# Graph network kernel: the first aggregation's low parts of the counts, replaced by two rows found on the chip

## What is computed

```python
h = jnp.maximum(_layernorm(x, axis=-1), 0.0)
x = x + _L1_gnn_ref(h, edge_index, W_l, b_l, W_r, gamma, beta)
# in it:
agg = jax.ops.segment_sum(x[src], dst, num_segments=n)
cnt = jax.ops.segment_sum(jnp.ones((src.shape[0],), x.dtype), dst, num_segments=n)
mean_agg = agg / jnp.maximum(cnt, 1.0)[:, None]
h = mean_agg @ W_l.T + b_l + x @ W_r.T
```

## Time and profile before

| | us |
|---|---|
| median of 3 runs | 393.89 |
| lowest, highest | 393.66, 395.64 |
| profiled execution, span | 394.1 |
| TensorE busy | 374.8 (95%) |
| VectorE busy | 312.1 (79%) |
| ScalarE busy | 171.6 (44%) |
| GpSimd busy | 4.2 (1%) |

### The profile page before, as it was taken

How to read it: one execution, slowest core, us unless ns; L and a number is a source line. 1 busy time by engine, 2 the same in 40 slices (tenths; PEclk the granted TensorE clock), 3 DMA queues, 4 the chain that set the end, 5 groups by cost and what they waited for, 6 DMA issues and landing times.

```text
span 394.1 us, 5108 instructions
## 1 busy us (share of the span) xinstructions
PE 374.8 (95%) x1786; PEld 282.2 (72%) x1786; DVE 312.1 (79%) x660; ACT 171.6 (44%) x287; POOL 4.2 (1%) x19
## 2 busy tenths in 40 slices
PE   2989999999999999999999999999999999999994
PEld 1545566666657888887678788887588878787773
DVE  5889999999848789897868976698875788388236
ACT  5664666563044234244559533262363530145410
POOL 4000000000000000000000000000000000000000
PEclk9999999999999999999999999999999999999988
DMA  7602444343135000068200512200600050000002
GB/s 238 250 1 69 152 154 141 105 153 112 52 112 183 1 2 0 2 215 315 111 2 1 172 43 101 114 0 0 211 4 0 2 180 33 2 0 0 2 12 94
DMA packets 16360, 32.92 MB, mean 84 GB/s; under 512 B 1360, under 2 KB 1488, under 8 KB 16336
## 3 DMA queue, kind: packets, MB, share of 16 engines
q1 hardware_dynamic: 15744, 32.25, 23.9%
q10 hardware_dynamic: 592, 0.36, 0.3%
HBM read 21.07 MB, written 1.05 MB: 56 GB/s over the span
## 4 chain that ended last, share of the span: by engine, by line
PE 77%; DVE 14%; ACT 4%; issue 2%; DMA 1%; DVEq 0%; ACTq 0%
PE acc L1395 11%; PE bank L1377 10%; PE bank L1480 7%; PE bank L1270 6%; PE bank L1271 6%; PE bank L1251 4%; PE acc L1251 4%; PE acc L1271 4%; PE acc L1270 4%; PE bank L1465 3%; PE acc L1451 3%; DVE big_rounded L652 2%; PE acc L1228 2%; PE bank L1228 2%; PE acc L1545 2%
## 5 line engine op out<-in xcount | busy, mean ns | idle before, releaser
L1395 PE MATMUL acc<-wide_rounded,c_rounded 128*126 128x512 f32 x200 | 59.5, 439 | 0.7 <-ACT acc L464 0.7
L1395 PEld LDWEIGHTS acc<-wide_rounded,c_rounded 128*126 128x126 f32 x200 | 36.9, 186 | 19.8 <-issue 13.0
L792 DVE TENSOR_SCALAR wide_rounded<-iota_f,picked 128x512 fp32r<-128x512 f32 x100 | 42.2, 480 | 1.5 <-issue 1.1
L483 ACT COPY z_sb<-acc 126x512 f32<-126x512 f32 x37 | 21.6, 585 | 42.0 <-PE acc L1395 33.3
L507 ACT ACTIVATE wide<-wide,low_col 128x512 f32<-128x512 f32 x32 | 21.3, 715 | 32.9 <-DVE low_col L905 32.8
L1480 PEld LDWEIGHTS bank<-v_sb,big 128*128 128x128 f32 x256 | 29.7, 192 | 4.7 <-issue 4.0
L625 DVE TENSOR_TENSOR wslot_rounded<-wslot,wide_rounded 128x512 fp32r<-128x512 f32 x24 | 16.2, 687 | 21.2 <-ACT wslot L377 21.2
L1480 PE MATMUL bank<-v_sb,big 128*128 128x65 f32 x256 | 31.6, 277 | 0.0
L798 DVE TENSOR_TENSOR c_rounded<-row_bc,wslot_rounded 128x1008 fp32r<-128x1008 bf16 x25 | 30.0, 1201 | 0.0
L1377 PE MATMUL bank<-t_sb,wslot 128*128 128x512 f32 x64 | 29.5, 594 | 0.5 <-ACT t_sb L459 0.5
L652 DVE TENSOR_TENSOR big_rounded<-big,big_rounded 128x1024 fp32r<-128x1024 f32 x24 | 29.1, 1221 | 0.5
(11 more groups left out here) (312 smaller groups left out, 769.6 us busy)
## 6 DMA issues: line engine op xcount, KB each, us to landing
big<-z_sb SPq DMA_DIRECT2D x36, 252.0 KB
big<-in_w SPq DMA_DIRECT2D x4, 2048.0 KB, 7.8
x_sb<-in_x SPq DMA_DIRECT2D x8, 256.0 KB, 4.6
big<-in_w_3t SPq DMA_DIRECT2D x2, 1024.0 KB, 6.7
row_bc<-in_rows SPq DMA_DIRECT2D x7, 256.0 KB, 6.4
wslot<-in_wq SPq DMA_DIRECT2D x1, 1024.0 KB, 8.9
wslot<-in_wk SPq DMA_DIRECT2D x1, 1024.0 KB, 10.7
wslot<-in_wv SPq DMA_DIRECT2D x1, 1024.0 KB, 12.8
```

Source lines behind the costliest of these rows:

```text
L483: nc.scalar.copy(stage[0:BROWS, b % STAGES, :], a).then_inc(S["staged"], 1)
L792: nc.vector.tensor_scalar(hot_ring[:, u, k, :], iota_f[:, :], picked[:, 0, s0 + k:s0 + k + 1], None, ALU.is_equal)
L1395: last = nc.tensor.matmul(to, st_ring[:, u, 2 * k + a, :, :].rearrange("p w k -> p (w k)"), hot_ring[:, u, k, :], start=False, stop=False, ...
```

## The change

A count below 4096 is exact in its rounded high part, so its low part is zero; since there are 8192 edges, at most two nodes can have a row in `c1` with a larger count. The change finds the numbers of these two rows on the chip and multiplies only their low parts. VectorE takes the largest count of each row (four maxima over 128x512) within the loop over `f`, and forms from them, with two tables of row numbers, one column for the first and one for the last such row. TensorE turns the two columns into rows, between the first and the second bank of `ff2` (`most_turn`). VectorE makes two distinct row numbers from 0 to 511 of them (`heavy_rows`, between the split of the counts and the loop over `t`). SyncE has stored the counts in a tensor in DRAM; it loads the two numbers into registers and fetches the two rows of counts. VectorE waits for them and splits them in parts, ahead of its loop over `t`. SyncE stores each high part of `h` in DRAM too, as it is made, and fetches the same two rows of it; GpSimd copies them, and TensorE adds four multiplies with two rows at the end of the aggregation, in place of 16 with 128 rows at its start. The fetches stand in SyncE's queue ahead of the load of `w1_2`. Ten new semaphores aside, this is the diff:

```diff
...
 TINY = 1e-37
+HEAVY, EXACT = 2, 4096
+assert (HEAVY + 1) * EXACT > E
...
         rcnt_sb = sb("rcnt_sb", [P, N])
+        most = sb("most", [P, NT])
+        row_no = sb("row_no", [P, HEAVY, NT])
+        heavy_no = sb("heavy_no", [P, HEAVY])
+        heavy_f = sb("heavy_f", [1, 2 * HEAVY])
+        heavy_i = sb("heavy_i", [1, HEAVY], I32)
         steps = rcnt_sb[:, 0:1 + SLOTS]
...
         c2_hi = t_lo
+        heavy_c, heavy_hi = row_bc[0:HEAVY, 0, :], row_bc_r[0:HEAVY, 1, :]
+        heavy_lo, heavy_h = row_bc_r[0:HEAVY, 2, :], row_bc_r[0:HEAVY, 1, :]
+        counts_kept = nc.dram_tensor("counts_kept", (N, N), F32, kind="Internal").ap()
+        highs_kept = nc.dram_tensor("highs_kept", (N, D), F32, kind="Internal").ap()
         c2_lo = both(lambda a: a[:, 0, :, :], wslot, wslot_r)
...
             load("w2_0", w2_0)
+            for t in range(NT):
+                sp.dma_start(counts_kept[t * P:(t + 1) * P, :], c1[:, t, :]).then_inc(S["counts_out"], 16)
             sp.wait_ge(S["ff1_mm"], FT)
...
             load("w_lr", wr_t, 1)
+            sp.wait_ge(S["heavy_ready"], 1)
+            _, heavy_rows = nc.values_load_multi_w_load_instructions(
+                heavy_i[0:1, :], engines=[mybir.EngineType.SP], min_val=0, max_val=N - 1,
+                skip_runtime_bounds_check_because="a row's number, bounded where it is made on the chip")
+            sp.wait_ge(S["counts_out"], 16 * NT)
+            for i in range(HEAVY):
+                sp.dma_start(heavy_c[i:i + 1, :], counts_kept[bass.ds(heavy_rows[i], 1), :]
+                             ).then_inc(S["heavy_c_in"], 16)
+            by, before_these, _, _ = parts["h1"]
+            for t in range(NT):
+                sp.wait_ge(S[by], before_these + t + 1)
+                sp.dma_start(highs_kept[t * P:(t + 1) * P, :], z_sb_r[:, t, :].bitcast(F32)).then_inc(S["highs_out"], 16)
+            sp.wait_ge(S["highs_out"], 16 * NT)
+            sp.wait_ge(S["heavy_parts"], 2)
+            for i in range(HEAVY):
+                sp.dma_start(heavy_c[i:i + 1, :], highs_kept[bass.ds(heavy_rows[i], 1), :]
+                             ).then_inc(S["heavy_h_in"], 16)
             sp.wait_ge(S["ff2_mm"], NT)
...
                            allow_small_or_imprecise_dtypes=True).then_inc(S["tables"], 2)
+            nc.gpsimd.iota(row_no[:, 0, :], [[P, NT]], base=1, channel_multiplier=1,
+                           allow_small_or_imprecise_dtypes=True).then_inc(S["row_numbers"], 1)
+            nc.gpsimd.iota(row_no[:, 1, :], [[-P, NT]], base=N, channel_multiplier=-1,
+                           allow_small_or_imprecise_dtypes=True).then_inc(S["row_numbers"], 1)
             nc.gpsimd.iota(need_c[:, :], [[0, 1]], base=-NBK, channel_multiplier=1,
...
                            allow_small_or_imprecise_dtypes=True).then_inc(S["tables"], 1)
+            pool.wait_ge(S["heavy_h_in"], 16 * HEAVY)
+            nc.gpsimd.tensor_copy(heavy_h, heavy_c).then_inc(S["heavy_h_ready"], 1)
         @block.scalar
...
+            def heavy_rows():
+                first, second = heavy_f[:, 0:1], heavy_f[:, 1:2]
+                same, other = heavy_f[:, 2:3], heavy_f[:, 3:4]
+                dve.wait_ge(S["most_turned"], 1)
+                link(nc.vector.tensor_reduce(heavy_f[:, 0:HEAVY],
+                                             bank[0][0:1, 0:HEAVY * P].rearrange("p (a n) -> p a n", a=HEAVY),
+                                             AX.X, ALU.max))
+                mark(nc.vector.tensor_scalar(first, first, -1.0, 0.0, ALU.add, ALU.max))
+                link(nc.vector.tensor_scalar(second, second, -1.0, float(N), ALU.mult, ALU.add))
+                link(nc.vector.tensor_single_scalar(second, second, float(N - 1), ALU.min))
+                mark(nc.vector.tensor_tensor(same, first, second, ALU.is_equal))
+                link(nc.vector.tensor_scalar(other, first, float(N // 2), -float(N), ALU.is_ge, ALU.mult))
+                link(nc.vector.scalar_tensor_tensor(out=other, in0=other, scalar=float(N // 2), in1=same,
+                                                    op0=ALU.add, op1=ALU.mult))
+                link(nc.vector.tensor_tensor(second, second, other, ALU.add))
+                nc.vector.tensor_copy(heavy_i[:, :], heavy_f[:, 0:HEAVY]).then_inc(S["heavy_ready"], 1)
             def on_diagonal(to, column):
...
                     weight_lo("w2_0", f - 2, f - 1)
+                    mark(nc.vector.tensor_reduce(most[:, f - 2:f - 1], c1[:, f - 2, :], AX.X, ALU.max))
+                elif f == 6:
+                    settle()
+                    dve.wait_ge(S["row_numbers"], HEAVY)
+                    link(nc.vector.scalar_tensor_tensor(
+                        out=row_no[:, :, :], in0=most[:, :].unsqueeze(1).broadcast_to([P, HEAVY, NT]),
+                        scalar=float(EXACT), in1=row_no[:, :, :], op0=ALU.is_ge, op1=ALU.mult))
+                    nc.vector.tensor_reduce(heavy_no[:, :], row_no[:, :, :], AX.X, ALU.max).then_inc(S["most_ready"], 1)
             settle()
...
                                         ALU.subtract).then_inc(S["c1_parts_ready"], 1)
+            heavy_rows()
+            dve.wait_ge(S["heavy_c_in"], 16 * HEAVY)
+            nc.vector.tensor_copy(heavy_hi, heavy_c).then_inc(S["heavy_parts"], 1)
+            dve.wait_ge(S["heavy_parts"], 1)
+            nc.vector.tensor_tensor(heavy_lo, heavy_c, heavy_hi.bitcast(F32), ALU.subtract
+                                    ).then_inc(S["heavy_parts"], 1)
...
                     last.then_inc(S[done], 1)
+                    if m == 0 and between:
+                        between()
...
             pe.wait_ge(S["ff1_ready"], NT)
+            def most_turn():
+                pe.wait_ge(S["most_ready"], 1)
+                pe.wait_ge(S["ff1_ready"], NT + 1)
+                for i in range(HEAVY):
+                    last = nc.tensor.transpose(bank[0][0:1, i * P:(i + 1) * P], heavy_no[:, i:i + 1], ident[:, :])
+                last.then_inc(S["most_turned"], 1)
             product_in_parts(hi, halves(wide_at, wide_lo, FT), weight("w2_0"), reads("ff_mid", FT), "ff2_mm",
-                             weight_lo="w2_0_lo")
+                             weight_lo="w2_0_lo", between=most_turn)
             pe.wait_ge(S["c1_parts_ready"], NT)
+            pe.wait_ge(S["heavy_ready"], 1)
             h1, c1s = halves(z_at, spare_at), halves(c1_hi, c1_lo)
...
                 pe.wait_ge(*reads("h1")[k][0])
-                for i in range(2):
-                    for m in range(NT):
-                        nc.tensor.matmul(bank[m][:, :], tile(h1[k][0], m), c1s[k][i], start=(k == 0 and i == 0),
-                                         stop=False)
+                for m in range(NT):
+                    nc.tensor.matmul(bank[m][:, :], tile(h1[k][0], m), c1s[k][0], start=(k == 0), stop=False)
             pe.wait_ge(S["h_ready"], 2 * NT)
...
                 for m in range(NT):
-                    last = nc.tensor.matmul(bank[m][:, :], tile(h1[k][1], m), c1s[k][0], start=False,
-                                            stop=(k == NT - 1))
-                    if k == NT - 1:
-                        last.then_inc(S["agg1_mm"], 1)
+                    nc.tensor.matmul(bank[m][:, :], tile(h1[k][1], m), c1s[k][0], start=False, stop=False)
+            pe.wait_ge(S["heavy_parts"], 2)
+            pe.wait_ge(S["heavy_h_ready"], 1)
+            for m in range(NT):
+                nc.tensor.matmul(bank[m][:, :], tile(heavy_h, m), heavy_lo, start=False, stop=True
+                                 ).then_inc(S["agg1_mm"], 1)
...
```

More of the change, by code:

```diff
@@ L96, in gnn_kernel @@
         wslot, wslot_r = sb_rounded("wslot", [P, 4, NT, D])
-        row_bc = sb("row_bc", [P, len(ROWS), D])
+        row_bc, row_bc_r = sb_rounded("row_bc", [P, len(ROWS), D])
         col = sb("col", [P, N_COLS])
@@ L226, in gnn_kernel @@
             "w_3_lo", "hi_scalar", "lo_vector", "wo_hi", "wo_lo", "base_ready",
-            "rcnt_ready", "dinv_ready", "c1_parts_ready", "loops_added", "c2_hi_ready", "mean_ready",
+            "rcnt_ready", "dinv_ready", "c1_parts_ready", "row_numbers", "most_ready", "most_turned", "heavy_ready", "counts_out", "highs_out",
+            "heavy_c_in", "heavy_h_in", "heavy_h_ready", "heavy_parts", "loops_added", "c2_hi_ready", "mean_ready",
             "out_done", "vector_order", "scalar_order", "pool_order", "consts", "tables",
```

2 lines of the change are left out of this document (1 added, 1 removed).

## The result

403.19 us (median of 4 runs, 401.58 to 404.61) against 394.58 us for the kernel before (4 runs, 393.66 to 395.64): ratio 1.0221, 95% interval 1.0193 to 1.0248, so 2.2% slower. The profiled execution has a span of 399.8 us; its own time was 401.58 us, the lowest of the four. The two profiled executions are not alike in one thing: in before's the clock fell near the end, while TensorE was still at work (rows 11 of before), in after's it did not. Later executions of the kernel before are of two kinds: of 55, 36 have a span of 391.9 to 392.5 us (the lower kind) and 19 one of 393.6 to 394.2 us (the upper kind). The profile shown of before, 394.1 us, is of the upper kind.

What follows compares the result with a forecast made beforehand. VectorE, without slack ahead of ff2's low terms, and its new wait for fetched rows were taken as the bound. Span 394.1 + 7.1 (delay) + 1.7 (clock) = 402.9, as a median 402.7 us; range 399.4 to 406.3.

Steps and rivals of the forecast that it cites:

- VectorE has no slack ahead of `ff2`'s low terms: Three maxima ahead of the last L652, for which TensorE waits, make the low terms 1.8 us later.
- The new wait of VectorE decides: Ahead of VectorE's loop over row tiles: small operations and the fetch make it start at 237.0 in place of 227.28.
- Four turns without waits: VectorE's loop over row tiles: its last turn begins 14.4 us after the first, at 251.4, long after ff2 ended.
- The second round trip is level with TensorE: Ahead of the two-row multiplies: heavy_h ready between 260.0 and 261.3, TensorE there at 260.9, so no wait.
- `w1_2` and the stores are covered: SyncE's queue: w1_2 lands at 264.9, asked for at 266.9, 2.0 us of cover; nobody but SyncE waits for the counts' store.
- The products with `w_lr` 7.1 us late with the clock held, 8.8 with its fall: Behind the aggregation on TensorE: products start at 261.8, 7.1 us late; the clock's fall behind two idle times adds 1.7 us.
- The sum: Whole kernel: 394.1 + 7.1 + 1.7 = 402.9 us, as a median 402.7 us, 2.2% slower.
- the sentence on the base: Kernel before: profiled execution has a span of 394.1 us, its runs a median of 393.89, 0.2 less.
- The lower bound of the range: Whole kernel: clock held, register load at its lower bound and faster small operations, 1.5 us less: 399.4 us.
- The held clock: Rival on TensorE's clock: VectorE's wait as told, but the clock doesn't fall, 401.0 us; chance 0.25.
- the round trips at their upper bounds: Rival on the fetches: landing 3.2 and register load 2.8 us, loop 2.7 us later, 406.3 to 408.0 us; chance 0.12.
- The covered wait: Rival at VectorE's loop: it starts by 230.2, ff2's end decides again, no change, 394 us; chance 0.07 with small losses.

Runs made afterwards that it cites:

- e1_maxima: Kernel before with only the four maxima over 128x512 added in VectorE's loop over f, results unused; 396.94 us, ratio 1.0064.
- e9_maxima_filled: Kernel of e1_maxima with 8 filler multiplies in TensorE's wait ahead of the low terms of ff2; 395.28 us, ratio 1.0036.
- e3_fetch_twice: Changed kernel with the two rows of counts fetched twice in series, VectorE waiting for both; 403.25 us, ratio 1.0238.
- e2_pool_parts: Changed kernel with the wait for the fetched rows of counts, and their split, moved from VectorE to GpSimd; 397.21 us, ratio 1.0058.
- e5_early_maxima: Changed kernel with the four maxima and two small operations moved ahead of the loop over f, into VectorE's idle time; 400.68 us, ratio 1.0174.
- e6_all: Changed kernel with maxima ahead of the loop over f, small operations in the first turn over t, rows split on GpSimd; 393.37 us, ratio 0.9972.
- e8_split_last_turn: Kernel of e6_all, but VectorE splits the fetched rows in its last turn over t and GpSimd only copies; 392.69 us, ratio 0.9967.
- e10_after_again: Changed kernel run once more, unedited; 402.33 us, ratio 1.0217.
- e4_keep_warm: Changed kernel with 9 and 14 filler multiplies in TensorE's two idle times between row tiles of the aggregation; 400.89 us, ratio 1.0149.

## Why the prediction was right, step by step

- *VectorE has no slack ahead of `ff2`'s low terms.* Right: 2.00 us of wait for a forecast of 1.8 on top of 0.20; e1_maxima shows it alone. What the forecast missed is that this wait can itself bring the clock down (e1_maxima against e9_maxima_filled: 1.6 us). Neither trace of the changed kernel shows such a fall. Where VectorE is as late and the clock did fall there (e3_fetch_twice), `ff2` ended at 245.37 and not 243.81, but the products followed the loop's delay, since VectorE is later still.
- *The new wait of VectorE decides.* Right, shown from three sides: taken away (e2_pool_parts), lengthened (e3_fetch_twice, by one profile), shifted (e5_early_maxima). The terms, forecast and measured: maxima 2.9 and 2.7 us, small operations 1.9 and 1.6, from `heavy_ready` to the rows 3.8 and 3.3, split 1.1 and 1.1. Within the trip the second issue was put too early (0.45 us behind the first, for 1.0) and the landing too long (2.2 for 1.3); 0.55 us too short against 0.9 too long, so that the errors cancel in part, by luck. Why the second issue came so late is open. An address from a register can't be the whole reason, since both issues of the second fetch, with the same registers, took 0.63 us together (L348). For the upper bound of the registers' load, 2.8 us, the prediction named no row; the load was 0.7. The prediction took the fixed 2.0 us of the Trainium skill ("DMA: Bandwidth & Descriptors", "Anatomy of one DMA") as a landing time. The page gives this figure for transfers that GpSimd issues, and this one was issued by SyncE; it landed 1.3 us behind its issue. The same page's rule on waiting late ("Rules for kernel authors") held: e6_all and e8_split_last_turn keep the trip and hide it.
- *Four turns without waits.* Right: 14.1 us for 14.4. The 4.9 us that the prediction read for one turn before (231.90 to 236.81) were not free of a wait: the next turn began just behind the end of its bank of `ff2` (236.77). Without one such turns take 4.73 us. TensorE's two idle times between the tiles were 2.46 and 3.54 us, for a forecast of 3.7 and 4.0, since the loop started earlier and `ff2` didn't end earlier by as much.
- *The second round trip is level with TensorE.* Wrong by its size, without effect: 4.6 us from the last high part to the end of GpSimd's copy, for 5.4 to 6.7, so the copy was done 3.5 us before TensorE came. The copy took 0.60 us, just under the 0.7 to 2.0 that the two nearest rows gave.
- *`w1_2` and the stores are covered.* Right, no wait.
- *The products with `w_lr` 7.1 us late with the clock held, 8.8 with its fall.* Measured 7.7 with the fall (7.4, and 0.25 for the earlier start), so the step was mis-sized by 1.1 us, as much as the start of the loop was; the errors behind it cancel. The fall came where it was put, between 248 and 257, and cost 1.5 us by the longer multiplies and turn (2.1 in the trace of e10_after_again), 1.3 to 1.6 by e4_keep_warm, for a forecast of 1.7.
- *The sum.* It came out at 402.7 for 403.19 (402.46 with all eight runs). That it is so close is luck, as errors cancel. The terms on the path were 1.1 us too large (8.8 for 7.7). From the lower kind of before, 393.9, the 7.4 us by which the products came later and the 0.2 to 0.3 us that the changed kernel needs more outside its span lead to 401.6, which is the time of the profiled execution (401.58). The other runs lie higher, up to 404.6. The trace of e10_after_again shows a fall of the clock where it costs 0.5 us more; the lower mean clock of the highest runs points to one fall more, which the sum did not have and no trace shows. And the sentence on the base was wrong: the span of 394.1 is not 0.2 us above the median; it belongs to an execution of about 395.6 us (spans of 394.1 go with 395.6 in the later runs), in which the clock had fallen near the end. The lower bound of the range is 0.1 off as well: 401.0 less 1.5 is 399.5.
- *Rivals.* The held clock (401.0) is what e4_keep_warm makes of it, 400.89; its products with `w_lr` come 6.1 us later than before and not 7.1, so this nearness is luck in part too. Of the round trips at their upper bounds nothing came: each was shorter than assumed. The covered wait is what e6_all and e8_split_last_turn build; with the maxima covered as well they are 0.6 and 1.2 us faster than before by the medians, some 1.3 to 1.5 us by the lower kind.

## What to carry to other kernels

Before work is put on an engine to spare another one, ask which instruction stands behind the new wait in that engine's own order; here a fetch of 4 KB in place of 2.7 us of multiplies held the loop that feeds TensorE. The same fetch holds nobody here when the engine that waits has nothing else to do (e2_pool_parts, e6_all), or waits late (e8_split_last_turn). And before a profile's span is used as a base, see of which kind the profiled execution is, and compare like with like.

## What the runs showed of the hardware

- A wait of TensorE of 2.0 us between busy stretches was enough to halve the clock for some 3.4 us (e1_maxima, clock 0.78, 0.50 and 0.87 in three slices of 2 us). The fall came when TensorE had gone on already, 1.5 us behind the end of the wait in e1_maxima and within 0.4 us in e2_pool_parts. It did not come in every execution: behind the same wait both traces of the changed kernel and that of e4_keep_warm show 1.00 from 222 to 230. With the wait filled it did not come in the one trace taken (e9_maxima_filled).
- The same idle times within the high multiplies of the aggregation cost 1.5 us of clock in one trace of the changed kernel and 2.1 in the other; it was at half for some 6.8 us in both, but 1.1 us later in the second, where more of TensorE's work lay in it.
- In 19 of 55 executions of the kernel before the span is some 1.6 us longer. Its profile, one of these, shows a fall of the clock with TensorE busy throughout (2.00 of 2 us in every slice from 370 to 382), behind eight multiplies with one row each (373.9 to 376.0). The changed kernel's first trace has the same eight (381.5 to 383.6) and no fall, so they are not enough by themselves; whether they are the reason was not tested.
- GpSimd's subtraction over 2x512 took 1.75 us in e2_pool_parts and 2.14 in e6_all. In e6_all VectorE's subtraction over 128x512 that started during it took 1.77 us instead of 0.69, and it took 0.69 again when GpSimd had no such work (e8_split_last_turn). In e2_pool_parts the same subtraction, started 0.1 us ahead of GpSimd's, took 0.69. These are one trace each.
- The fetch of two rows of 2 KB by register from DRAM took 3.3 us from the numbers in SBUF to the rows in SBUF, in both traces of the changed kernel and in e5_early_maxima; 1.3 us of it is the landing behind the second issue.
